# Decay masks of a delta rule: written by ScalarE as scaled copies instead of by GpSimd

## What is computed

```python
def step(S, inp):
    qt, kt, vt, gt, bt = inp
    S = S * jnp.exp(gt)[..., None, None]
    v_adj = (vt - jnp.einsum('bhk,bhkv->bhv', kt, S)) * bt[..., None]
    S = S + kt[..., None] * v_adj[..., None, :]
    o = jnp.einsum('bhk,bhkv->bhv', qt, S)
    return (S, o)
```

## Time and profile before

| | |
|---|---|
| runs | 2406.59, 2410.67, 2412.37 us; median 2410.67 |
| profiled execution | 2405.05 us, its span 2403.3 |
| delta rule, about 77 to 1575 us | 33 steps of 43.9 to 47.7 us |
| busy over the span | TensorE 2092.2 us (87%), VectorE 1859.5 (77%), ScalarE 1433.9 (60%), GpSimd 1004.2 (42%) |
| `g_mask` on GpSimd, L1188 | 132 instructions, 161.0 us, mean 1251 ns |
| taps on VectorE, L958 | 384 instructions, 338.0 us, mean 893 ns |
| GpSimd idle ahead of `r_norm` (L1202), until VectorE's `sumsq` | 517.3 us in 32 steps |
| granted TensorE clock, mean | 0.954 of full speed |

### The profile page before, as it was taken

One profiled execution on the slowest core, in us unless ns is written; L12 is line 12 of the kernel. 1 busy time (PEld: TensorE's weight loads), 2 busy tenths in 40 slices (PEclk: granted clock), 3 DMA queues, 4 the chain that ended last, 5 costly groups with the idle time before them and its releaser, 6 DMA issues. The chain is left out here.

```text
span 2403.3 us, 56028 instructions
## 1 busy us (share of the span) xinstructions
PE 2092.2 (87%) x19224; PEld 1530.1 (64%) x19224; DVE 1859.5 (77%) x4187; ACT 1433.9 (60%) x3914; POOL 1004.2 (42%) x938
## 2 busy tenths in 40 slices
PE   5799999999999999998999999858988999756998
PEld 2576776776777777776777776645656666524444
DVE  8777877887777887777877877636888888764997
ACT  2466666666666666666666666536776777633333
POOL 7434334334234334234334234213566666650332
PEclk8799999999999999999999999769999999987999
DMA  2100000000000000000000000053333333113111
GB/s 73 49 9 22 30 9 22 31 9 22 31 9 22 31 9 22 31 9 22 31 9 22 31 9 22 19 164 90 97 97 90 94 85 96 52 44 121 56 55 51
DMA packets 122857, 107.56 MB, mean 45 GB/s; under 512 B 12080, under 2 KB 97072, under 8 KB 122800
## 3 DMA queue, kind: packets, MB, share of 16 engines
q1 hardware_dynamic: 122800, 106.87, 14.3%
HBM read 72.24 MB, written 34.60 MB: 44 GB/s over the span
## 5 line engine op out<-in xcount | busy, mean ns | idle before, releaser
L601 PE MATMUL proj<-xn_hi,w_lo 128*128 x768 | 362.6, 472 | 0.0
L958 DVE SCALAR_TENSOR_TENSOR qkv<-conv_in,taps,qkv 128x512 f32<-128x512 f32 x384 | 338.0, 893 | 8.9 <-ACT qkv L830 8.9
L602 PE MATMUL proj<-xn_lo,w_hi 128*128 x768 | 307.4, 400 | 0.2 <-issue 0.2
L603 PE MATMUL proj<-xn_hi,w_hi 128*128 x768 | 306.1, 399 | 0.0
L1202 POOL TENSOR_TENSOR r_norm<-sumsq,neg_half 128x8 f32<-128x8 f32 x32 | 67.3, 2102 | 517.3 <-DVE sumsq L1118 517.3
L1173 POOL TENSOR_TENSOR o_pow<-o_var,neg_half 128x4 f32<-128x4 f32 x68 | 89.4, 1332 | 412.6 <-DVE o_var L990 412.6
L1068 DVE TENSOR_TENSOR i_less_r<-bank_c,join_mask 128x256 f16<-128x256 f32 x330 | 124.4, 417 | 113.3 <-PE bank_c L666 112.9
L884 ACT ACTIVATE inv<-bank_b 128x256 f16<-128x256 f32 x330 | 111.5, 382 | 161.7 <-PE bank_b L686 161.4
L603 PEld LDWEIGHTS proj<-xn_hi,w_hi 128*128 128x128 f32 x768 | 146.1, 190 | 35.4
L601 PEld LDWEIGHTS proj<-xn_hi,w_lo 128*128 128x128 f32 x768 | 146.0, 190 | 25.9
L1188 POOL TENSOR_TENSOR g_mask<-mask_ge,gates 128x512 fp32r<-128x512 f32 x132 | 161.0, 1251 | 0.3 <-POOLq L506 0.3
(11 more groups left out here) (288 smaller groups left out, 6103.1 us busy)
## 6 DMA issues: line engine op xcount, KB each, us to landing
out_t<-o_out SPq DMA_DIRECT2D x68, 256.0 KB, 2.0
o_raw<-out_t SPq DMA_DIRECT2D x32, 512.0 KB, 5.4
w_raw<-in_L_attn_W_qkv_dram SPq DMA_DIRECT2D x36, 256.0 KB, 2.8
wq_dram<-wq_q SPq DMA_DIRECT2D x48, 128.0 KB, 1.8
w_raw<-in_L_attn_W_z_dram SPq DMA_DIRECT2D x18, 256.0 KB, 2.7
x_sb<-in_x_dram SPq DMA_DIRECT2D x16, 256.0 KB, 2.7
x_in<-in_x_dram SPq DMA_DIRECT2D x16, 256.0 KB, 5.8
wq_raw<-in_L_ffn_w_gate_dram SPq DMA_DIRECT2D x16, 256.0 KB, 2.6
```

Of the source, the lines that this page charges most:

```text
L601: pe.matmul(out, w_lo[:, k, cols], sh.xn_hi[:, k, tok], start=(k == 0), stop=False)
L602: pe.matmul(out, w_hi[:, k, cols], sh.xn_lo[:, k, tok], start=False, stop=False)
L603: product = pe.matmul(out, w_hi[:, k, cols], sh.xn_hi[:, k, tok], start=False, stop=(k == KT - 1))
L958: dve.scalar_tensor_tensor(out=out, in0=conv_in[:, j, :, k:k + T], scalar=taps[:, j, k:k + 1], in1=out, op0=ALU.mult, op1=ALU.add).then_in ...
```

## The change

The masks of step n+1 are written by ScalarE in step n, after the z tile (`tile_copy(n, 4)`) and ahead of the weight split 3 and of `v_r`. They are 16 copies of 128x128 a step, each scaled by a column of gates. The columns come from a new small tile, `g_cols`, which VectorE copies at the head of the step. GpSimd's four multiplications go, and so does its wait. The first masks follow ScalarE's six weight splits and use zero columns, since step 0 has no projected data.

```diff
+        g_cols = sb("g_cols", [P, 2, 8], F32)
@@ decay_sums (TensorE)
-                        pe.wait_ge(mask_done[s], 2 * n + 2)
+                        pe.wait_ge(mask_done[s], n + 1)
@@ ScalarE
+                def mask_gates(n, copied):
+
+                    for s in S:
+                        if copied is not None:
+                            act.wait_ge(cols_done, copied)
+                            act.wait_ge(d_ps[s], copied)
+                        for i in range(2):
+                            for hb in range(4):
+                                last = act.activation(g_mask[s][:, i, hb, :], sh.mask_ge[:, :], ACT.Copy,
+                                                      scale=g_cols[:, s, 4 * i + hb:4 * i + hb + 1])
+                        last.then_inc(mask_done[s], 1)
...
                         tile_copy(n, 4)
+                        mask_gates(n + 1, n + 1)
                         if next_g is not None:
                             split(next_g, 3)
...
                 for j in range(TILES):
                     split(0, j)
+                mask_gates(0, None)
@@ VectorE
                 def step(n, project, next_g):
+                    if project:
+                        dve.wait_ge(mask_done[1], n + 1)
+                        dve.tensor_copy(g_cols[:, :, :], sh.gates[:, bass.ds(2 * n + 2, 2), 8:16]).then_inc(cols_done, 1)
@@ GpSimd
-                def mask_gates(n):
-                    for s in S:
-                        for i in range(2):
-                            g_cols = sh.gates[:, bass.ds(2 * n + s, 1), 8 + 4 * i:12 + 4 * i].rearrange("p a h -> p (a h)")
-                            pool.tensor_tensor(g_mask[s][:, i, :, :], bcast(sh.mask_ge[:, :], 1, 4), bcast(g_cols, 2, P),
-                                               ALU.mult).then_inc(mask_done[s], 1)
...
-                        for s in S:
-                            pool.wait_ge(d_ps[s], n + 1)
-                        mask_gates(n + 1)
...
-                mask_gates(0)
```

## The result

The median went from 2409.18 us (2406.59 to 2412.37) to 2391.51 us (2388.98 to 2393.04), a measured ratio of 0.9931 with an interval of 0.9919 to 0.9943 (the two medians alone give 0.9927). The median before is of four runs, the three listed before the change and one more of 2407.70. The profiled executions ran 2405.05 and 2390.52 us, with spans of 2403.3 and 2388.8, so 14.5 us of the 17.7 are to be found in the two traces.

A forecast was written before the change was run, and what follows sets the result against it. Different engines limit different stretches; TensorE waits at level 2 for VectorE taps slowed by GpSimd's masks. 6.8 + 14.0 + 8.4 - 3.8 - 4.5 = 20.9 us gain, from 2410.67 to 2389.8, predicted as 2389; range 2376 to 2397, outer high end 2406.

The forecast's parts named there:

- the forecast's range: Whole kernel: forecast with its bounds 2376 to 2397 us, chance 0.58; outer high end 2406.
- Weight steps: Eight last steps of key heads, which split weights: 14.0 us gained at level 2, 8.4 from six clock dips gone.
- Ordinary steps: Level 2 of the other projecting steps: 0.31 us gained in each of 22, 6.8 us in all.
- ScalarE's sixteen copies: Between the z tile and v_r: a block of 4.6 us, hidden in ScalarE's wait, cost 0 in each step.
- turns into a loss from about 6.4: Rival, ScalarE late before the second v_r: a longer block delays TensorE, 2419 us; chance 0.08.
- The copy at the head: VectorE's 128x16 copy at each step's head: cost 0.12 us a step, 3.8 in all, bounds 2.2 to 9.6.
- The first masks: Before step 0, after ScalarE's sixth weight split: later scores and kk_diag cost 4.5 us, between 2.9 and 6.5.
- The first steps of a head: First step of each key head: two of eight lose about 2.1 us to the clock; left unchanged, 4.2 either way.
- The rival that the falls only move: Clock dips leave weight steps but fall elsewhere: 2397.4 us, or 2401.6 with two more in first steps; chance 0.22.

The follow-up runs named there:

- e_nomask: Kernel before, with GpSimd's masks left out of the steps and no engine doing that work: 2383.54 us, ratio 0.9893.
- e_both: Changed kernel, with GpSimd also writing four masks at their old place into tiles nobody reads: 2409.97 us, ratio 1.0007.
- e_block24: Changed kernel with eight more scaled ScalarE copies a step, into a tile nobody reads: 2409.52 us, ratio 1.0012.
- e_cols: Changed kernel with VectorE's copy of the gate columns moved from the step's head to behind the first tap: 2387.92 us, ratio 0.9923.
- e_first: Changed kernel without the sixteen copies ahead of step 0; GpSimd zeroes the first masks instead: 2389.62 us, ratio 0.9935.
- e_best: Changed kernel with gate-column copy and split 4 moved, first masks zeroed by two ScalarE copies ahead of the loops: 2386.50 us, ratio 0.9915.
- e_heads_before: Kernel before, with VectorE's weight splits 4 and 5 moved into the next head's first step: 2414.51 us, ratio 1.0037.
- e_split4: Changed kernel with weight split 4 moved earlier in the weight step, on ScalarE and VectorE: 2384.25 us, ratio 0.9910.
- e_block20: Changed kernel with four more scaled ScalarE copies a step, into a tile nobody reads: 2389.12 us, ratio 0.9918.
- e_heads: Changed kernel with VectorE's weight splits 4 and 5 moved into the next head's first step: 2405.98 us, ratio 0.9994.
- e_best2: Changed kernel with gate-column copy moved behind the first tap and weight split 4 moved earlier: 2381.01 us, ratio 0.9896.
- e_late: Kernel before, with GpSimd's masks kept but started only after the step's SiLU: 2432.83 us, ratio 1.0112.

## Why the prediction came out as it did

The time, 2391.51 against 2389, fell inside the forecast's range, and faster was right; the gain was 17.7 us against the sum's 20.9. Two slips of its arithmetic changed nothing: the sum gives 2389.8, not 2389, and the low end of the range starts from 2384.2, the profiled execution, where the high end starts from the runs without a profile. Point by point:

- *Weight steps.* I had 14.0 for the level and 8.4 for the clock, 22.4, less 0.12 x 8 for the copy, so 21.4. The trace shows 21.8. Level 2 is 2.78 us, no wait for `i_less_r` is left, and all eight clocks are 1.00. e_nomask gives the same length (44.57), and e_both brings the 1.6 us wait back. Shown. The weight step's other wait, 1.40 us for `diag`, is there before and after, and alone it brought no fall; I had written that ordinary steps have the same waits, but theirs is 0.63.
- *Ordinary steps.* The price of 0.31 was right (43.87 - 43.56 in e_nomask), the count was not. I took 24 less two; but eight of those 24 are the first steps of a head, and there are 16 ordinary ones. These gave 3.6 us net, where 16 x (0.31 - 0.12) is 3.0.
- *ScalarE's sixteen copies.* 4.78 us against 4.6, at no cost to the steps, right. The room behind them is larger than I had it: against my "some 5.7" 6.0 is still hidden, and against my "turns into a loss from about 6.4" the 7.1 us of e_block24 stand about where the kernel before does (1.0012). My row of four at 0.28 each fits better than the 0.42 of one alone. The Trainium skill, ScalarE: Activation LUTs, section What ACT_TABLE_LOAD costs, led to 4.7 us; 4.78 agrees.
- *The copy at the head.* 0.12 taken for each step; `kk_diag` moved by 0.07, and e_cols gave back 0.08 in an ordinary step, nothing in a weight step and 0.2 in the first of a head. That is about 2.7 us in all instead of 3.8.
- *The first masks.* 4.5 taken, mis-sized. The first scores moved by 6.0 us (77.51 to 83.52), `kk_diag` by 4.1 (80.96 to 85.03, where I had 4.9), and the first inverse by as much; but step 1 began only 2.5 later, and I had bounded it at 2.9 from below. The rest came behind the first inverse, where I had not looked: TensorE had waited 2.21 us ahead of it and ran at the lower clock behind it, and now waits 0.32 (the step's mean is 0.96, from 0.93). TensorE in step 0, before and after:

```profile
87.71 0.75 PE L650 MATMUL bank_b<-ident,inv_t 64*64 64x64 f16 x16 [2.21 <-issue]
...
89.84 1.72 PE L640 MATMUL bank_a<-ident,qkv 128*128 128x128 f32 x8
```

```profile
91.79 0.64 PE L652 MATMUL bank_b<-ident,inv_t 64*64 64x64 f16 x16 [0.32 <-issue]
...
93.17 1.03 PE L642 MATMUL bank_a<-ident,qkv 128*128 128x128 f32 x8
```

- *The first steps of a head: the step that failed.* I wrote "I leave these as they are", with a bound of 4.2 either way. Six of seven now lose the clock instead of two (my "two of eight" had overlooked step 0, at 0.93), and the group became 5.1 us longer, where without more falls it would be some 0.6 shorter (45.24 to 45.16 in a step that keeps the clock). The rival that the falls only move came half true: they left the weight steps, as forecast, and came up in the first steps. In e_nomask this happened without any new work or wait, so what set it off is the relief. Two over-estimated costs (the start by 2.0, the head copy by 1) stand against it. The 3.4 us after the delta rule come on top of it in the profiled span, which gained 14.5 us where the medians gained 17.7. That the total came so near is in part luck: the falls I had not counted and the costs I had counted too high are of like size.

What decides that the clock falls is open. The table of runs shows a pattern: with falls in weight steps, few or fewer come in first steps (6 and 2, 6 and 1), and with none in weight steps nearly all first steps have one (6 or 7 of 7); e_first, e_best and e_heads_before break it. The length of TensorE's wait alone does not decide: 2.67 us gave two of seven in the kernel before, 2.63 gave seven of seven in e_nomask, 2.25 seven of seven in e_split4, and 2.97 one of seven in e_block24. In the changed kernel seven like steps with waits of 2.86 to 2.90 gave six falls, and the one that kept the clock is the first of them; in e_block20 it is the second. The Trainium skill, TensorE: Matmul & The Clock Gate, section What's actually happening, has activity judged on a free-running beat, by which a wait's place in time would matter; these counts are in keeping with that, but no run here tests it apart, since none shifts the steps without changing them.

## What to carry to other kernels

GpSimd operations beside VectorE operations that read two SBUF tiles about doubled their time in both places measured here (1.40 to 2.90 us, 2.19 to 4.50), so the price of such an operation depends on its place and not on its own length alone; price it at the engine that waits for VectorE (here TensorE, 0.3 us of 1.5 in an ordinary step and all of it in a weight step). Work that another engine can take into a wait it already has is free up to a threshold that can be measured by adding more of the same (here between 6.0 and 7.1 us). When a wait leaves one kind of step, read the granted clock of the neighbouring steps too, for the falls may only change their place.

## What the runs showed that I had not expected

- Where an engine's outer loop goes round, it can stand for 2.2 to 3.2 us with nothing to wait for ("issue"), once per head, seven times. This came when VectorE's loop over heads got a third copy of a step (17.7 us in all in e_heads and in e_heads_before), and on ScalarE when sixteen instructions ahead of its loop were taken away (16.1 us in e_first, 21.1 in e_best), though its loop was that of the changed kernel and of e_best2. In each of these four runs, and in no other, the instruction packets of the page rose, from 29 to 31 up to 64 or 66, about 5 for each of seven passes. That instructions are fetched anew at that place is my reading of it; that the size and the position of the code decide is argued from these four runs, and not tried further.
- Eight VectorE operations of 128x128 took 4.50 us instead of 2.19 beside GpSimd's masks, a larger loss than that of the taps (two in 2.90 instead of 1.40), while GpSimd's four took 4.13 there, 4.92 beside the taps, and 4.04 in the step at 622 us, away from both. Which operands decide was not tried.
- A fall of the clock comes in sizes: beside a first step that keeps it (45.16 us in the changed kernel), one with a mean of 0.96 takes 1.2 to 1.4 us more, and one of 0.93 takes 2.3 more; e_late has one of 0.90, 4.1 more than its like (50.24 against 46.1).
- The part behind the delta rule, the same in all kernels, took 875.0 to 881.1 us in the profiled executions. Differences of some us between two profiled spans are to be read step by step.
